# Handing the routed activations to the down projection through memory and block transposes instead of four TensorE transposes

## The reference

```python
flat_idx = top_k_index.reshape(-1)                  # T*K choices, T = 8192, K = 8
sort_idx = jnp.argsort(flat_idx)
xs = jnp.repeat(x, K, axis=0)[sort_idx]             # rows sorted by expert
gate = jax.lax.ragged_dot(xs, w_gate, group_sizes)  # (T*K, 1024) x (1024, 512) of the row's expert
up = jax.lax.ragged_dot(xs, w_up, group_sizes)
down = jax.lax.ragged_dot(jax.nn.silu(gate) * up, w_down, group_sizes)   # x (512, 1024)
unsort = jnp.argsort(sort_idx)
routed = (down[unsort].reshape(T, K, H) * tkw[..., None]).sum(axis=1)
```

## Time and profile before

| what | us |
|---|---|
| median of 3 runs | 12066.55 |
| lowest and highest run | 12063.37, 12068.08 |
| the profiled execution's own time | 11994.11 |
| its span, first to last instruction | 11992.5 |
| TensorE busy in the span | 11729.8 (98%) |
| VectorE busy | 4965.2 (41%) |
| ScalarE busy | 2385.8 (20%) |
| GpSimd busy | 4292.6 (36%) |

### The profile page before, as it was taken

The page is one execution under the profiler, slowest core; times in us unless marked ns, Lnnn a source line. Parts: engine busy times, 40 slices in busy tenths (PEclk is TensorE's granted clock), DMA queues, the critical chain, the costliest instruction groups (busy, mean ns, idle before and its releaser), DMA issues.

```text
span 11992.5 us, 202804 instructions
## 1 busy us (share of the span) xinstructions
PE 11729.8 (98%) x53248; PEld 9606.0 (80%) x53249; DVE 4965.2 (41%) x6781; ACT 2385.8 (20%) x3042; POOL 4292.6 (36%) x4236
## 2 busy tenths in 40 slices
PE   8999799999999999999999999999999999999998
PEld 7888577777788888888888888888887788888887
DVE  5666655554333333333433343333434434333332
ACT  2112233332111111111211121121212212111111
POOL 2555432221333333333333333333333333333333
PEclk9999799999999999999999999999999999999999
DMA  4333222222333333333433343343435434333332
GB/s 160 131 132 135 89 87 94 88 93 85 81 63 82 83 63 84 84 82 86 104 62 84 63 105 84 62 103 63 104 89 149 109 62 125 63 62 82 62 63 56
DMA packets 698920, 1068.09 MB, mean 89 GB/s; under 512 B 460882, under 2 KB 461074, under 8 KB 675704
## 3 DMA queue, kind: packets, MB, share of 16 engines
q0 software_dynamic: 212608, 622.54, 23.9%
q1 hardware_dynamic: 486136, 443.39, 11.6%
HBM read 614.06 MB, written 451.44 MB: 89 GB/s over the span
## 4 chain that ended last, share of the span: by engine, by line
PE 72%; issue 1%; DVE 1%; DMA 0%; DVEq 0%; SPq 0%; ACT 0%; POOL 0%; ACTq 0%; POOLq 0%
PE pg L66 8%; PE pg L68 8%; PE pg L67 8%; PE pd L68 8%; PE pd L66 8%; PE pd L67 8%; PE pu L68 8%; PE pu L66 8%; PE pu L67 8%; PE ta L1956 2%; DVE w_lo L1854 0%; DVEq L1577 0%; DMA xq<-xn_rows,idx_q 0%; ACT w_hi L1787 0%; POOL xq L1740 0%
## 5 line engine op out<-in xcount | busy, mean ns | idle before, releaser
L1740 POOL DMA_INDIRECT xq<-xn_rows,idx_q x2120 | 2188.6, 1032 | 935.5 <-issue 485.1
L1748 POOL DMA_INDIRECT out_rows<-y,idx_s x528 | 860.7, 1630 | 4630.3 <-issue 4613.3
L66 PE MATMUL pg<-w_hi,x_hi 128*128 128x512 f32 x4224 | 1701.6, 403 | 46.9 <-DVE x_lo L1870 40.6
L68 PE MATMUL pg<-w_hi,x_lo 128*128 128x512 f32 x4224 | 1654.0, 392 | 0.0
L66 PE MATMUL pd<-w_hi,a_hi 128*128 128x512 f32 x4224 | 1644.5, 389 | 6.6 <-DVEq L1895 6.6
L67 PE MATMUL pg<-w_lo,x_hi 128*128 128x512 f32 x4224 | 1648.9, 390 | 0.0
L68 PE MATMUL pd<-w_hi,a_lo 128*128 128x512 f32 x4224 | 1645.5, 390 | 0.0
L67 PE MATMUL pd<-w_lo,a_hi 128*128 128x512 f32 x4224 | 1643.7, 389 | 0.0
L66 PE MATMUL pu<-w_hi,x_hi 128*128 128x512 f32 x4224 | 1643.2, 389 | 0.0
L67 PE MATMUL pu<-w_lo,x_hi 128*128 128x512 f32 x4224 | 1643.2, 389 | 0.0
L68 PE MATMUL pu<-w_hi,x_lo 128*128 128x512 f32 x4224 | 1643.1, 389 | 0.0
(11 more groups left out here) (293 smaller groups left out, 15590.5 us busy)
## 6 DMA issues: line engine op xcount, KB each, us to landing
stage<-in_w_all SPq DMA_DIRECT2D x174, 1024.0 KB, 10.1
quads<-slot_table SPq DMA_DIRECT2D x2120, 1.0 KB
xq<-xn_rows,idx_q POOLq DMA_INDIRECT x2120
xt<-in_x SPq DMA_DIRECT2D x64, 512.0 KB, 4.4
xn_rows<-xn SPq DMA_DIRECT2D x64, 512.0 KB, 2.6
xn_turned<-sx_hi SPq DMA_DIRECT2D x64, 512.0 KB, 3.1
xn_turned<-sx_lo SPq DMA_DIRECT2D x64, 512.0 KB, 3.0
out_rows<-bases SPq DMA_DIRECT2D x64, 512.0 KB, 3.3
```

What stands on the lines that cost most here:

```text
L66: m(dst, hi, whi[:, cols], start=begin, stop=False)
L68: return m(dst, lo, whi[:, cols], start=False, stop=end)
L1740: g.indirect_dma_start(out=xq[q][:, n], out_offset=None, in_=xn_q, in_offset=bass.IndirectOffsetOnAxis(ap=idx_q[q][:, n:n + 1], axis=0))\
L1748: g.indirect_dma_start(out=out, out_offset=bass.IndirectOffsetOnAxis(ap=idx_s[q][:, 0:1], axis=0), in_=y[q][:], in_offset=None, compute_op ...
```

## The change

The four TensorE transposes, the identity they need, and their PSUM tile go. In their place ScalarE, once `av` is ready, issues four DMAs of 32 partitions each (4 pieces of 512 bytes from each partition) that write the tile's activations to a scratch tensor in memory, waits for all four, and issues one DMA that reads it back with 2 KB for each of the 128 partitions into `aq`. VectorE turns `aq` in 32x32 blocks into `aT`, and `a_hi` and `a_lo` are made from `aT`. The features then stand on the partitions in a fixed other order, and the host lays the rows of the down weights in that order (`terms`). The lists of ScalarE and VectorE are changed to fit: x of tile t+1 comes first, then the activations and down weights of t-1.

```diff
@@ GpSimd
-            g.memset(ident[:], 0.0).then_inc(ident_made, 1)
...
@@ ScalarE
+            def store_activated(t):
+                act.wait_ge(av_ready, t + 1)
+                for n in range(4):
+                    a.dma_start(a_d.rearrange("(a j g c) -> g j a c", a=4, j=32, g=4)[n],
+                                av[32 * n:32 * n + 32].rearrange("j (a c) -> j a c", a=4)).then_inc(a_stored, 16)
+
+            def load_activated(t):
+                act.wait_ge(a_stored, t * 64 + 64)
+                wait_past(act, a_turned, t)
+                a.dma_start(aq[:].rearrange("p g c -> p (g c)"), a_d.rearrange("(p c) -> p c", p=P))\
+                    .then_inc(a_loaded, 16)
+
             def a_high(t):
-                act.wait_ge(ta_done, t + 1)
-                a.activation(a_hi[:], ta[:], ACT.Copy).then_inc(ah_ready, 1)
+                act.wait_ge(a_turned, t + 1)
+                wait_past(act, down_done, t * 2)
+                a.activation(a_hi[:].rearrange("p b (g j) -> p b g j", g=4),
+                             aT[:].rearrange("p (g b j) -> p b g j", g=4, b=KI), ACT.Copy).then_inc(ah_ready, 1)
...
             def begin(t):
-                a_high(t - 1)
                 if isinstance(t, int):
                     down_high(t - 1)
                 else:
...
+                a_high(t - 1)
 
             def tile(t, q):
-                if not (isinstance(t, int) and t == 0):
+                begun = not (isinstance(t, int) and t == 0)
+                if begun:
+                    load_activated(t - 1)
+                x_high(t + 1, 1 - q)
+                if begun:
                     begin(t)
-                x_high(t + 1, 1 - q)
                 act.wait_ge(gate_done, t + 1)
...
+                store_activated(t)
                 with act.If(value_of(act, fresh, t + 1, 1) > 0):
                     run = value_of(act, runs, t + 1, E)
                     act.wait_ge(up_done, t + 1)
@@ VectorE
             def turn_rows(t, q, half):
                 dve.wait_ge(gathered[q], half * 64 + 64)
-                wait_past(dve, xh_ready, t)
+                wait_past(dve, xl_ready, t)
...
+            def turn_activated(t):
+                dve.wait_ge(a_loaded, t * 16 + 16)
+                v.transpose(aT[:], aq[:].rearrange("p g c -> p (g c)")).then_inc(a_turned, 1)
+
             def a_low(t):
                 dve.wait_ge(ah_ready, t + 1)
-                v.tensor_tensor(a_lo[:], ta[:], a_hi[:], ALU.subtract).then_inc(al_ready, 1)
+                v.tensor_tensor(a_lo[:].rearrange("p b (g j) -> p b g j", g=4),
+                                aT[:].rearrange("p (g b j) -> p b g j", g=4, b=KI),
+                                a_hi[:].rearrange("p b (g j) -> p b g j", g=4), ALU.subtract).then_inc(al_ready, 1)
...
             def begin(t):
-                a_low(t - 1)
+                turn_activated(t - 1)
...
                 dve.sem_inc(down_weights, 1)
+                a_low(t - 1)
 
             def tile(t, q):
                 half = (t - q) // 2
                 begun = not (isinstance(t, int) and t == 0)
+                turn_rows(t + 1, 1 - q, half + q)
+                x_low(t + 1, 1 - q)
                 if begun:
                     begin(t)
-                turn_rows(t + 1, 1 - q, half + q)
-                x_low(t + 1, 1 - q)
...
-                wait_past(dve, ta_done, t)
+                wait_past(dve, a_stored, t * 64)
                 v.tensor_tensor(av[:], pu[:], sg[:], ALU.mult).then_inc(av_ready, 1)
@@ TensorE
                 if not (isinstance(t, int) and t == 0):
                     down(t - 1)
-                pe.wait_ge(av_ready, t + 1)
-                for i in range(KI):
-                    last = nc.tensor.transpose(ta[:, i], av[:, i * P:(i + 1) * P], ident[:])
-                last.then_inc(ta_done, 1)
@@ host
+    def terms(w):
+        return w.reshape(E, 4, KI, P // 4, H).transpose(0, 2, 1, 3, 4).reshape(E, I, H)
+
+    down = np.concatenate([terms(w_down), sw_down.reshape(SH, I, H)])
```

More of the change, by code:

```diff
@@ L1580, in expert_stage @@
 def expert_stage(nc, T, io, plan):
-    (xn_d, out, table, w_all) = io
+    (xn_d, out, table, w_all, a_d) = io
     starts, experts, fresh, runs, kinds = plan
@@ L1606, in expert_stage @@
         quarter = sb("quarter", [P, 1])
-        ident = sb("eident", [P, P])
         idx_s = [sb(f"idx_s{i}", [P, 2], I32) for i in range(2)]
@@ L1616, in expert_stage @@
         av = sb("av", [P, I])
+        aq = sb("aq", [P, 4, I // 4])
+        aT = sb("aT", [P, I])
         y = [sb(f"y{i}", [P, H]) for i in range(2)]
@@ L1619, in expert_stage @@
         pu = pb("pu", [P, I])
-        ta = pb("ta", [P, KI, P])
         pd = [pb(f"pd{i}", [P, 512]) for i in range(2)]
@@ L1627, in expert_stage @@
         idx_loaded = [sem(f"idx_loaded{i}") for i in range(2)]
-        ident_made = sem("ident_made")
+        quarters_set = sem("quarters_set")
         pool_passed = sem("pool_passed")
@@ L1636, in expert_stage @@
         turned = sem("turned")
-        ta_done = sem("ta_done")
+        a_stored = sem("a_stored")
+        a_loaded = sem("a_loaded")
+        a_turned = sem("a_turned")
         down_done = sem("down_done")
@@ L1754, in tile @@
                     add(t - 1, 1 - q, half - 1 + q)
-            g.memset(ident[:], 0.0).then_inc(ident_made, 1)
-            pool.wait_ge(ident_made, 1)
-            g.affine_select(out=ident[:], in_=ident[:], compare_op=ALU.not_equal, fill=1.0, base=0,
-                            pattern=[[-1, P]], channel_multiplier=1).then_inc(ident_made, 1)
             for n in range(4):
-                pool.wait_ge(ident_made, 2 + n)
-                g.memset(quarter[32 * n:32 * n + 32], float(n)).then_inc(ident_made, 1)
-            pool.wait_ge(ident_made, 6)
+                if n:
+                    pool.wait_ge(quarters_set, n)
+                g.memset(quarter[32 * n:32 * n + 32], float(n)).then_inc(quarters_set, 1)
+            pool.wait_ge(quarters_set, 4)
             for q in range(2):
@@ L1953, in tile @@
                     down(t - 1)
-                pe.wait_ge(av_ready, t + 1)
-                for i in range(KI):
-                    last = nc.tensor.transpose(ta[:, i], av[:, i * P:(i + 1) * P], ident[:])
-                last.then_inc(ta_done, 1)
-            pe.wait_ge(ident_made, 2)
             through(pe, pe_passed, tile, lambda t, q: down(t - 1))
@@ L1969, in build @@
     z_d = nc.dram_tensor("z_rows", [D, (NC + 2) * (C + 2)], F32, kind="Internal").ap()
+    a_d = nc.dram_tensor("activated", [P * I], F32, kind="Internal").ap()
     table = nc.dram_tensor("slot_table", [rows, 2], I32, kind="Internal").ap()
@@ L1985, in build @@
         plan_stage(nc, T, cnt_base, plan, plan_d)
-        expert_stage(nc, T, (xn_d, A["out"], table, A["w_all"]), plan)
+        expert_stage(nc, T, (xn_d, A["out"], table, A["w_all"], a_d), plan)
 def layouts(x, ln_w, ln_b, in_proj_W, conv_w, conv_b, x_proj_W, dt_proj_W, dt_proj_b, A_log, D_param, out_proj_W,
@@ L2004, in layouts @@
     up = np.concatenate([quarters(w_up), halves(sw_up)])
-    down = np.concatenate([w_down, sw_down.reshape(SH, I, H)])
+    def terms(w):
+        return w.reshape(E, 4, KI, P // 4, H).transpose(0, 2, 1, 3, 4).reshape(E, I, H)
+    down = np.concatenate([terms(w_down), sw_down.reshape(SH, I, H)])
     n = E + SH
```

## The result

The changed kernel takes **12101.8 us** (median of 8 runs, 12093.3 to 12108.3), the kernel before 12064.2 (8 runs, 12059.8 to 12068.1): ratio 1.003 with an interval of 1.0019 to 1.0041. It is 38 us (0.3%) slower. The time lies inside the range of 11860 to 12130, but I had said 12009, faster, and gave slower 0.20. By its price the third of the four rivals came about: over all 28 changes of expert one costs 10.2 us, more than the 8.6 from which the gain is eaten.

What follows compares the result with a forecast made beforehand. TensorE, busy 98% of the span, was taken to bound the kernel. The sum -242 + 164 + 20 = -58 us gave 12009 us from 12066.55; the range meant to hold 8 in 10 was 11860 to 12130.

Steps and rivals of the forecast that it cites:

- rival 3: Changes of expert: late stores beside weight loads make one cost over twice as much; at 10 us each, 12125; chance 0.12.
- Saving: TensorE between down and gate: removing the transposes saves 0.46 us in each of 527 tiles, 242 us.
- The slow first step: From first to second gate matmul, 0.32 us where 0.227 is the rule; expected to go with the transposes.
- Steady tile: Ordinary tiles: VectorE's and ScalarE's new work stays hidden with 4 us to spare; steps become 16.32 to 16.35 us.
- Rival 2: Every tile, between ScalarE's stores and `aT`: the trip through memory is too long, giving 12536; chance 0.08.
- Change of expert: Where a fresh expert begins: three stalls from list order, together 5.9 us at each of 28 changes, 164 us more.
- up weights: Before up at a change: stores waiting for `av` delay ScalarE's `w_hi`, then `w_lo`; TensorE waits 2.5 us.
- activations of t: Before down at a change: VectorE's chain behind the up weights' `w_lo` ends at `a_lo` late; 2.3 us.
- down weights: One tile after a change: down weights' `w_lo`, then `a_lo`, ready at 12.0 against 10.88; 1.1 us.
- stated span of 11940 to 12110: Forecast alone, with bounds for the stores' issue, the saving's lower end and the 20 us added for one-tile places.
- One-tile experts: Four places where experts of one tile follow each other: 20 us added for all three delays and slower clock, bounds 0 and 60.
- My bound on idle time: Expert stage: the prediction is wrong if TensorE's idle time grows by less than 80 or more than 240 us.

Runs made afterwards that it cites:

- experiment 10: Changed kernel with the load of the activations issued, waited for and issued again: 12267.2 us against 11990.6 for the kernel before, ratio 1.0231.
- 9: Changed kernel with ScalarE and VectorE doing the activations ahead of x and of down's `w_lo`, stores still early: 12090.4 us against 11990.6 before, ratio 1.0083.
- experiment 5: Kernel before, transposes and lists kept, also making the trip into an unread buffer, stores behind the up weights: 12072.0 us against 12050.7, ratio 1.0017.
- experiment 7: Changed kernel with stores behind the up weights and down weights first in ScalarE's list, ahead of `aT` in VectorE's: 11836.3 us against 11990.6 before, ratio 0.9872.
- 1: Kernel before without the four transposes and without the trip, so down gets a wrong operand: 11815.7 us against 12065.2, ratio 0.9793.
- 2: Changed kernel with ScalarE's four stores moved behind the up weights' `w_hi`: 11986.0 us, ratio 0.9938 to the kernel before.
- 8: As experiment 7, but with the stores ahead of the up weights again: 12025.1 us against 12050.7 for the kernel before, ratio 0.998.
- 6: As experiment 5, but with the stores ahead of the up weights: 12179.2 us, ratio 1.0108 to the kernel before.
- 4: Kernel before, transposes kept and no trip, with only the change's order of ScalarE's and VectorE's lists: 12151.2 us, ratio 1.0073 to the kernel before.

## Why the prediction was right or wrong

**Saving: right.** I had 0.46 a tile, 242 us; it is 0.491, 259, and the run without the trip gives 249 in all. The slow first step (0.32 where 0.227 is the rule) went with the transposes, and a little more than the two rows showed. The length of a transpose would have given more than twice that; the starts were the right thing to read. Of the Trainium skill (TensorE: Matmul & The Clock Gate, Part 4: PE-mode transpose) this leaves the 275 ns true as a length; as a price the trace contradicts it.

**Steady tile: right.** The step is 16.32, and `aT` waits 9 times in 528. A longer trip (experiment 10) and a stricter place for it (9) leave the median where it is. Rival 2 doesn't come about in quiet tiles.

**Change of expert: the mechanism right, two of three terms too small.** This is where the prediction failed: the price of a change, 5.9 us. The clean change costs 8.1:

| term | forecast | measured | why |
|---|---|---|---|
| up weights | 2.5 | 3.7 | `av` done at 15.5 of the tile, not 15.0; stores 1.80 as said; branch behind them 1.3, not 0.79 |
| activations of t | 2.3 | 2.2 | as said; only 0.28 of it is idle time, since up ran partly at 1.2 GHz |
| down weights | 1.1 | 2.1 | `xT` starts 0.9 behind `y`, not 0.15; `w_lo` starts 0.6 behind the first `w_hi`, not at once; the branch ahead of `w_hi` is 0.4, not 0.8 |

Most of the 2.2 more is hand-overs and branches, which I had taken from the cheapest rows that I had seen. (The stated span of 11940 to 12110 also left out 40 of the 60 us that I had allowed the one-tile places; with them it ends at 12150.) The activations' term is the same chain under either clock: VectorE's list set the pace, so a slower up filled the idle time without adding to it.

**What I had as a rival and not in the sum** is smaller: 18 changes at 8.1 are 146 of the 170 us, and some are dearer than the clean one (mean 9.4, median 8.6). 18 of these 24 us lie at the five changes in which the stores landed latest, while weights move. From the last store's issue to the load's it is 2.7 us in the median of 497 tiles, and 5.0, at most 8.3, in the 31 tiles in which weight loads are in flight (worked out from the starts of both in the trace). One such case, ScalarE's and VectorE's timelines with SP's four weight loads issued at 4706.5 to 4708.6 (their row first):

```profile
4706.47 2.14 SPq L1685 DMA_DIRECT2D stage<-in_w_all  x4
```

```profile
4718.06 1.76 ACTq L1798 DMA_DIRECT2D activated<-av  x4
4726.23 0.34 ACTq L1804 DMA_DIRECT2D aq<-activated  x1
4726.69 1.06 ACT L1790 ACTIVATE x_hi<-xT 128x1024 fp32r<-128x1024 f32 x1 [13.26 <-DMA activated<-av]
```

```profile
4732.34 0.71 DVE L1896 STREAM_TRANSPOSE aT<-aq 128x512 f32<-128x512 f32 x1 [3.34 <-DMA aq<-activated]
```

6.4 us pass between the last store's end and the load. `x_hi` starts 1.1 us later in its tile than in the median one, the rest of its 13.26 is idle time of every tile; `aT` waits 3.34 for the load behind it, and the change costs 12.6 instead of 8.1. That is the step that rival 3 names, at a few changes. The Trainium skill (DMA: Bandwidth & Descriptors, Issuing engines are not separate DMA queues) says that DMAs issued by different engines run on the same 16 DMA engines and interleave. This trace agrees: 2.7 without weight loads, 5.0 with them. But in experiment 5, where ScalarE makes the same trip and waits up to 7.9 us for its stores, and down doesn't depend on them, all of it costs 21 us. A late landing seems to be dear where down waits for the trip as well. Experiment 10 shows such a wait; that the dependence is what sets 5 apart is argued, since 5 also keeps its lists and its transposes.

**One-tile experts: too small.** I had 10 changes at 5.9 and 20 for clock and closeness, 79; it is 117 (174 less the 58 that they exceed by before). The windows of the kernel after over the clean change and over one of these places (columns as above):

```profile
10222.00:10245.00 23.00, 19.16 (x77) 15.05 (x76) 11.18 (x11) 5.89 (x5) 6.37 (x6) 0.93 0.37 80
9352.00:9464.00 112.00, 80.05 (x289) 62.62 (x288) 59.13 (x44) 38.31 (x28) 23.84 (x19) 0.85 0.59 183
```

Of the 112 us TensorE is idle 32, and the granted clock is 0.85, so that a part runs at 1.2 GHz; VectorE is busy 53%, so it isn't full, and what is lost is lost in waits. In one tile of 39.9 us `w_hi` waited 12.35 us for `stage`, whose loads SP had issued only at 9416.4: the delay had reached the loads too. Before, this tile exceeds its step by 14.6 us already, with the change by 23.6. Which part of the 117 is that and which the clock wasn't taken apart.

**The clock: missing in the prediction's own test.** I had it only in the 20 us. Busy time shows 101 us of longer matmuls in the whole stage: TensorE is at 1.2 GHz behind the waits, as in the clean change, whose window has 0.93; there eight matmuls in a row stand 0.43 us apart instead of 0.227. The time at 1.2 GHz in the stage, worked out from the clock's records, is 85 us before, 158 in experiment 7, 290 in the change and 473 in experiment 10, and rises with the excess (48, 146, 345, 574). 205 us more at half the clock are 102 us of work, which fits the 101. That doesn't make the clock a term of its own. In the clean change 1.9 us of slower matmuls filled a wait that VectorE's list would have made anyway, and only 0.3 of the 8.1 us is clock beyond the chain. How much it adds elsewhere isn't shown. My bound on idle time, "by less than 80 or more than 240", would have let the result pass: idle time grew by 198. By leaving out the clock it tested too little.

The sum again, with measured terms: saving -259 for -242, longer experts' changes +170 for 106, one-tile places +117 for 79, start +5 for 0. That is +33 in place of -58, within 8 us of the stage's 41; the difference is in steps a little under the median before (5) and in the last tile (3). Between forecast and stage lie 98 us: 64 at the 18 changes (40 from the two small terms, 24 from dearer changes), 38 in the one-tile places, 13 at the start and in the remainder, less 17 for the larger saving.

**Shown**: that the transposes' time is gained whole (1); that the stores' place costs 107 to 128 us, in three pairs (change and 2, 8 and 7, 6 and 5); that the order of x, activations and down weights costs 64 and 75 us (change and 8, 2 and 7), and 86 with the transposes still there (4); that the trip with late stores costs 21 where down doesn't depend on it (5). **Argued only**: how much of the 101 us of clock adds to the time and how much fills waits; why late landings cost more in the change than in experiment 5; and how much of a late landing is contention at the memory and how much at the DMA engines. The lists alone (86) and the early trip alone (129) make 215 of the 287 us; no run takes the other 72 apart.

## What to carry to other kernels

A DMA that is issued from a compute engine's list is an instruction of that list: ask what it waits for, and what stands behind it that doesn't depend on it; here weight blocks that were ready stood behind `av`, and moving one call by seven lines is worth 116 us, three times the whole change. When a step leaves the bound engine, the price is in the stretches in which the helping engines are full, not in the average tile; find those stretches, count the serial chain there with its branches and hand-overs, and allow for slower matmuls behind each new wait. Small terms taken from the cheapest rows are low: sum a chain of eight with the median row, and give the range the upper one.

## What the runs showed of the hardware that I had not expected

- A transpose of 128x128 fp32 takes 273 ns by its row and a quarter of 0.49 us in the stream: leaving four of them out made the step 0.49 shorter, and the 0.36 between first transpose and first gate matmul did not show all of it.
- From the last 64 KB store's issue to the load that waits for all four it is 2.7 us, and 5.0 in the median while another queue loads weights (DMA share 0.80 in 4717 to 4727, 0.49 in the stage). A load of 256 KB that is issued behind 4 MB of weight loads takes 9.0 us to its last packet instead of 2.3.
- Issue on ScalarE: 1.80 us for four stores of 128 pieces each, 0.34 for the load of one piece a partition.
- The same kernel before takes 12064, 12051 or 11991 us in different jobs, with the same stage of the routed experts in the two traces of it. In the traces of all kernels the stages ahead end either at 3076 to 3098, with 233 to 253 us at 1.2 GHz in them, or at 3014 to 3019 with 193 to 204. So a difference below half a per cent is read only against runs of the same job.
